# A slot-attention stage in new order: projections in other PSUM banks, ScalarE's and VectorE's queues rearranged

## The reference, cut to what matters

```
xn = layernorm(x);  q, k, v = rope(xn @ Wq), rope(xn @ Wk), xn @ Wv
sk = clip(xn @ sk_w1 @ sk_w2 + sk_b2, -32, 32);  wk = exp(sk);  zk = cumsum(wk over time)
sv = clip(xn @ sv_w1 @ sv_w2 + sv_b2, -32, 32);  wv = exp(sv);  zv = cumsum(wv over time)
logits = (causal(q k^T) @ wk) * scale / zk;      p = softmax(logits over the 64 slots)
o = causal((p / zv) @ wv^T) @ v
g = xn @ Wg;   on = o * rsqrt(mean(o*o) + eps) * gnorm_w
x = x + (on * g * sigmoid(g)) @ Wo
```

## Time and profile before

| | us |
|---|---|
| time of the kernel, median of 3 runs (lowest, highest) | 1716.53 (1711.35, 1729.82) |
| the profiled execution's own time | 1712.71 |
| its span, first to last instruction | 1710.9 |
| first stage, up to its last instruction | about 302.4 of 1710.9 |
| PE busy over the span | 1504.7 (88%) |
| ScalarE, VectorE, GpSimd busy | 1257.0, 1190.1, 530.2 |

### The profile page before, as it was taken

How to read it: one execution, slowest core, us unless ns; L and a number is a source line. 1 busy time by engine, 2 the same in 40 slices (tenths; PEclk the granted TensorE clock), 3 DMA queues, 4 the chain that set the end, 5 groups by cost and what they waited for, 6 DMA issues and landing times. The chain is left out here.

```text
span 1710.9 us, 37885 instructions
## 1 busy us (share of the span) xinstructions
PE 1504.7 (88%) x14142; PEld 724.0 (42%) x14142; DVE 1190.1 (70%) x1933; ACT 1257.0 (73%) x2113; POOL 530.2 (31%) x908
## 2 busy tenths in 40 slices
PE   7889987774699999998889999978874999999998
PEld 4666666662133333336633333345541333333356
DVE  4778777798999999967710000047878999999743
ACT  4654563697488888885689999926663888888863
POOL 3422342552323333334400010022221333333362
PEclk9999998797699999999999999989986999999999
DMA  4000000025434444420133333211333333333211
GB/s 132 1 1 2 1 2 1 1 82 166 142 102 111 107 110 111 107 62 27 45 89 98 94 100 97 66 36 39 99 108 113 84 91 89 89 92 92 67 38 38
DMA packets 140411, 125.42 MB, mean 73 GB/s; under 512 B 38411, under 2 KB 118341, under 8 KB 140229
## 3 DMA queue, kind: packets, MB, share of 16 engines
q1 hardware_dynamic: 130980, 121.90, 24.6%
q0 software_dynamic: 8192, 0.77, 0.9%
q10 hardware_dynamic: 1056, 0.33, 0.1%
HBM read 77.19 MB, written 44.96 MB: 71 GB/s over the span
## 5 line engine op out<-in xcount | busy, mean ns | idle before, releaser
L1700 ACT ACTIVATE m_probs<-m_psum 128x512 f32<-128x512 f32 (+1 forms) x768 | 511.6, 761 | 60.9 <-PE m_psum L1623 59.9
L1700 ACT ACTIVATE e_probs<-e_psum 128x512 f32<-128x512 f32 x512 | 276.4, 596 | 53.6 <-PE e_psum L1623 52.0
L1740 DVE TENSOR_REDUCE a_minus_max<-m_psum 128x2 f32<-128x1024 f32 x256 | 300.8, 1218 | 14.4 <-PE m_psum L1632 13.1
L1740 DVE TENSOR_REDUCE a_minus_max<-e_psum 128x2 f32<-128x1024 f32 x256 | 300.5, 1218 | 14.8 <-PE e_psum L1632 13.3
L1623 PE MATMUL m_psum<-m_q_stack,m_k_stack 114*32 114x512 bf16 (+1 forms) x4096 | 294.3, 384 | 6.6 <-DMA m_k_stack<-n_parts 4.4
L1643 PE MATMUL m_psum<-m_probs,m_v_ones 128*32 128x512 f32 x2048 | 269.5, 599 | 3.9 <-DVE m_pair L1690 2.6
L1623 PEld LDWEIGHTS m_psum<-m_q_stack,m_k_stack 114*32 114x32 bf16 (+1 forms) x4096 | 106.4, 96 | 224.2 <-issue 124.6
L1623 PE MATMUL e_psum<-e_q_stack,e_k_stack 126*32 126x512 bf16 x2048 | 157.5, 384 | 2.3 <-ACT e_probs L1700 2.2
L1643 PE MATMUL e_psum<-e_probs,e_v_ones 128*32 128x512 f32 x1024 | 132.2, 593 | 0.0
L1632 PE MATMUL m_psum<-m_k_stack,m_q_stack 48*128 48x512 bf16 x512 | 93.2, 400 | 31.8 <-DVE a_minus_max L1740 24.3
L1632 PE MATMUL e_psum<-e_k_stack,e_q_stack 60*128 60x512 bf16 x512 | 93.9, 400 | 29.4 <-DVE a_minus_max L1740 23.6
(11 more groups left out here) (402 smaller groups left out, 2630.3 us busy)
## 6 DMA issues: line engine op xcount, KB each, us to landing
polar_q<-m_late SPq DMA_DIRECT2D x24, 256.0 KB, 3.0
polar_k<-m_late SPq DMA_DIRECT2D x24, 256.0 KB, 3.2
m_q_stack<-polar_q SPq DMA_DIRECT2D x64, 96.0 KB, 2.3
m_k_stack<-polar_k SPq DMA_DIRECT2D x64, 96.0 KB, 2.4
ctx<-a_context_pairs SPq DMA_DIRECT2D x48, 128.0 KB
a_context_pairs<-slot_w SPq DMA_DIRECT2D x24, 256.0 KB, 2.2
m_q_stack<-dist_parts SPq DMA_DIRECT2D x192, 32.0 KB
m_k_stack<-dist_parts SPq DMA_DIRECT2D x192, 32.0 KB
```

The source lines that it names most:

```text
L1700: act.activation(self.buf.probs[(NT * m + c) % self.buf.PROBS][:, self.WIDE * part:self.WIDE * (part + 1), :], self.ps_s[i % self.PAIRS], ...
L1740: dve.tensor_reduce(self.minus_max[n % 2][:, k:k + NT + 1:NT], self.ps_r[r % self.TWOS], AX.X, ALU.max, negate=True).then_inc(self.two_fre ...
```

## The change: what it does

Banks: projections 1 and 3 use bank 7, projections 0 and 2 bank 4; "low" uses bank 7, "gT" bank 4; the slot matmuls stay in 0 to 3, but all four belong to batch s (lag 0). PE: in each step, projections 1 and 0 come right after `attend`, projections 3 and 2 between the two halves of the logits, `low` ahead of `outputs`, slots 1 and 0 after `mean_squares`, slots 3 and 2 after `project_out`, and the gate's matmul last. A step opens with the key sums; `turn_q` goes ahead of `turn_k`; the transposes of the norm go behind `turn_values`. ScalarE: the logarithm and the copy of the first key sums come first in the step, ahead of the softmax's exponential; then the copies of q and k, the values' logarithm and inverse, and behind these the four gate activations (the sigmoid is split into methods of its own, with the same instructions); the four qkv copies and the low copy come before `square`; the four exponentials of w end the step. VectorE: the clips move to the end of the step before, `gate_product` behind the third state copy, the statistics of the next batch between `key_newton` and `scale_logits`, `apply_gate` ahead of `add`, the second scan to the very end. GpSimd's and SyncE's queues are as before. No instruction is added or dropped.

```diff
@@ -1938,12 +1938,18 @@
-    def gate_sigmoid(self, act, b):
+    def gate_exponential(self, act, b):
         act.wait_ge(self.g_steps, 3 * b + 1)
         act.activation(sig[:, :], sig[:, :], ACT.Exp, scale=-1.0, bias=self.consts[:, 1:2]).then_inc(self.g_steps, 1)
+
+    def gate_logarithm(self, act, b):
+        sig = self.sig[b % 2]
         act.wait_ge(self.g_steps, 3 * b + 2)
         act.activation(sig[:, :], sig[:, :], ACT.Ln, bias=self.sv.ones[:, 0:1]).then_inc(self.g_steps, 1)
+
+    def gate_sigmoid(self, act, b):
+        sig = self.sig[b % 2]
         act.wait_ge(self.g_steps, 3 * b + 3)
         act.activation(sig[:, :], sig[:, :], ACT.Exp, scale=-1.0).then_inc(self.sig_ready, 1)
...
-        slot = SlotAttention(nc, sv, tag, norm, last_slot=3)
+        slot = SlotAttention(nc, sv, tag, norm, last_slot=2)
         banks = Banks(nc, tag, 8, (
-            ("slot2", 2, 1, (slot.clip_done[2],)), ("slot3", 3, 1, (slot.clip_done[3],)), ("zk0", 5, 1, (slot.zk_ready[0],)),
-            ("state1", 7, 1, (slot.state_ready[1],)), ("kT", 5, 1, (slot.kT_ready,)), ("qT", 6, 1, (slot.qT_ready,)),
+            ("zk0", 5, 1, (slot.zk_ready[0],)), ("state1", 7, 1, (slot.state_ready[1],)), ("kT", 5, 1, (slot.kT_ready,)), ("qT", 6, 1, (slot.qT_ready,)),
...
-            ("L1", 6, 1, (slot.lg_ready[1],)), ("L0", 5, 1, (slot.lg_ready[0],)), ("proj1", 1, 0, (slot.qkv_ready[1],)),
-            ("o", 4, 2, (slot.on_ready,)), ("proj0", 0, 0, (slot.qkv_ready[0],)), ("wvT1", 6, 1, (slot.wvT_ready[1],)),
-            ("ms", 5, 2, (slot.ln_ready,)), ("out", 6, 3, (slot.x_done,)), ("proj3", 3, 0, (slot.qkv_ready[3],)), ("proj2", 2, 0, (slot.qkv_ready[2],)),
-            ("low", 4, 0, (slot.lowT_ready,)), ("gT", 5, 0, (slot.gated_ready,)), ("slot1", 1, 0, (slot.clip_done[1],)), ("slot0", 0, 0, (slot.clip_done[0],))))
+            ("proj1", 7, 0, (slot.qkv_ready[1],)), ("proj0", 4, 0, (slot.qkv_ready[0],)), ("L1", 6, 1, (slot.lg_ready[1],)),
+            ("proj3", 7, 0, (slot.qkv_ready[3],)), ("proj2", 4, 0, (slot.qkv_ready[2],)), ("L0", 5, 1, (slot.lg_ready[0],)), ("low", 7, 0, (slot.lowT_ready,)),
+            ("o", 4, 2, (slot.on_ready,)), ("wvT1", 6, 1, (slot.wvT_ready[1],)), ("ms", 5, 2, (slot.ln_ready,)),
+            ("slot1", 1, 0, (slot.clip_done[1],)), ("slot0", 0, 0, (slot.clip_done[0],)), ("out", 6, 3, (slot.x_done,)),
+            ("slot3", 3, 0, (slot.clip_done[3],)), ("slot2", 2, 0, (slot.clip_done[2],)), ("gT", 4, 0, (slot.gated_ready,))))
         norm.banks = slot.banks = banks
...
         for s in STEPS:
             for b in batch(s, 1):
-                slot.slot(pe, b, 2)
-                slot.slot(pe, b, 3)
                 slot.key_sums(pe, b, 0)
                 slot.states(pe, b, 1)
+                slot.turn_q(pe, b)
                 slot.turn_k(pe, b)
-                slot.turn_q(pe, b)
                 slot.states(pe, b, 2)
                 slot.scores(pe, b)
...
-            for b in batch(s, 0):
-                norm.turn(pe, b)
             for b in batch(s, 1):
                 slot.states(pe, b, 3)
                 slot.key_sums(pe, b, 1)
                 slot.turn_values(pe, b, 0)
+            for b in batch(s, 0):
+                norm.turn(pe, b)
             for b in batch(s, 2):
                 slot.attend(pe, b)
+            for b in batch(s, 0):
+                slot.project(pe, b, 1)
+                slot.project(pe, b, 0)
             for b in batch(s, 1):
                 slot.slot_logits(pe, b, 1)
+            for b in batch(s, 0):
+                slot.project(pe, b, 3)
+                slot.project(pe, b, 2)
+            for b in batch(s, 1):
                 slot.slot_logits(pe, b, 0)
             for b in batch(s, 0):
-                slot.project(pe, b, 1)
+                slot.low(pe, b)
             for b in batch(s, 2):
                 slot.outputs(pe, b)
-            for b in batch(s, 0):
-                slot.project(pe, b, 0)
             for b in batch(s, 1):
                 slot.turn_values(pe, b, 1)
             for b in batch(s, 2):
                 slot.mean_squares(pe, b)
+            for b in batch(s, 0):
+                slot.slot(pe, b, 1)
+                slot.slot(pe, b, 0)
             else:
                 for b in batch(s, 3):
                     slot.project_out(pe, b)
             for b in batch(s, 0):
-                slot.project(pe, b, 3)
-                slot.project(pe, b, 2)
-                slot.low(pe, b)
+                slot.slot(pe, b, 3)
+                slot.slot(pe, b, 2)
                 slot.gate(pe, b)
-                slot.slot(pe, b, 1)
-                slot.slot(pe, b, 0)
         folding.turn_ternary(pe, 0)
...
         for s in STEPS:
             for b in batch(s, 1):
-                slot.qkv_copy(act, b, 2)
-                slot.low_copy(act, b)
-                slot.gate_guard(act, b)
-                slot.gate_sigmoid(act, b)
-                slot.weights(act, b, 1)
-                slot.weights(act, b, 0)
+                slot.key_log(act, b, 0)
             for b in batch(s, 2):
                 slot.exponential(act, b)
             for b in batch(s, 1):
-                slot.weights(act, b, 2)
-                slot.key_log(act, b, 0)
+                slot.q_copy(act, b)
+                slot.k_copy(act, b)
             for b in batch(s, 2):
                 slot.value_log(act, b)
+                slot.value_inverse(act, b)
             for b in batch(s, 1):
-                slot.k_copy(act, b)
-                slot.q_copy(act, b)
+                slot.gate_guard(act, b)
+                slot.gate_exponential(act, b)
+                slot.gate_logarithm(act, b)
+                slot.gate_sigmoid(act, b)
             for b in batch(s, 0):
                 norm.normalise(act, b)
             for b in batch(s, 1):
-                slot.weights(act, b, 3)
-            for b in batch(s, 2):
-                slot.value_inverse(act, b)
-            for b in batch(s, 1):
                 slot.key_log(act, b, 1)
                 slot.values_copy(act, b, 0)
-                slot.key_inverse(act, b)
             for b in batch(s, 0):
                 norm.copy(act, b)
+            for b in batch(s, 1):
+                slot.key_inverse(act, b)
+            for b in batch(s, 0):
+                slot.qkv_copy(act, b, 1)
+                slot.qkv_copy(act, b, 0)
+                slot.qkv_copy(act, b, 3)
+                slot.qkv_copy(act, b, 2)
+                slot.low_copy(act, b)
             for b in batch(s, 2):
                 slot.square(act, b)
-            for b in batch(s, 0):
-                slot.qkv_copy(act, b, 1)
             for b in batch(s, 1):
                 slot.values_copy(act, b, 1)
             for b in batch(s, 2):
                 slot.inverse_rms(act, b)
             for b in batch(s, 0):
-                slot.qkv_copy(act, b, 3)
-                slot.qkv_copy(act, b, 0)
+                slot.weights(act, b, 1)
+                slot.weights(act, b, 0)
+                slot.weights(act, b, 3)
+                slot.weights(act, b, 2)
         folding.finish_proj(act)
...
+        norm.statistics(dve, 0)
+        norm.aggregate(dve, 0)
+        dve.wait_ge(constants, ALL_CONSTANTS)
+        dve.wait_ge(memsets, 3)
         for s in STEPS:
-            for b in batch(s, 0):
-                norm.statistics(dve, b)
-                norm.aggregate(dve, b)
-            if s == 0:
-                dve.wait_ge(constants, ALL_CONSTANTS)
-                dve.wait_ge(memsets, 3)
             for b in batch(s, 1):
-                slot.clip(dve, b, 1)
-                slot.clip(dve, b, 0)
-                slot.gate_product(dve, b)
-                slot.clip(dve, b, 2)
-            for b in batch(s, 2):
-                slot.scan(dve, b, 1)
-            for b in batch(s, 1):
-                slot.clip(dve, b, 3)
                 slot.state_copy(dve, b, 1)
...
             for b in batch(s, 1):
                 slot.state_copy(dve, b, 3)
+                slot.gate_product(dve, b)
                 slot.mask_scores(dve, b, 1)
                 slot.mask_scores(dve, b, 2)
             for b in batch(s, 2):
                 slot.mask_attention(dve, b, 1)
                 slot.mask_attention(dve, b, 2)
                 slot.mask_attention(dve, b, 0)
+                slot.mask_attention(dve, b, 3)
             for b in batch(s, 1):
                 slot.key_newton(dve, b)
+            for b in batch(s + 1, 0):
+                norm.statistics(dve, b)
+                norm.aggregate(dve, b)
+            for b in batch(s, 1):
                 slot.scale_logits(dve, b, 1)
-            for b in batch(s, 2):
-                slot.mask_attention(dve, b, 3)
...
                 slot.scan(dve, b, 0)
             for b in batch(s, 2):
                 slot.apply_rms(dve, b)
+            for b in batch(s, 0):
+                slot.clip(dve, b, 1)
+                slot.clip(dve, b, 0)
+            for b in batch(s, 2):
```

(8 more changed lines are left out.)

## The result

The changed kernel takes 1703.17 us (median of 8 runs, 1702.03 to 1704.43), the kernel before 1714.72 (8 runs): a ratio of 0.9923, 95% interval 0.9896 to 0.9949. The forecast was 1706, within 1696 to 1722, and less than 1% faster. The intervals of the ratios are 0.1 to 0.3% to either side, up to 5 us. So a difference between two of the variants further down rests on the length of the step in their traces, and the times only agree with it. The profiled span went from 1710.9 to 1701.6 us. The last instruction of the first stage, the sum at L2454 (L2460 in the changed file), starts at 301.68 before and at 290.21 after, 11.5 us earlier; the later groups gave back 2.2 in these two executions (9.3 in the whole span).

What follows compares the result with a forecast made beforehand. The prediction took PE's queue, with its waits, to bound the first stage's step. Its terms -2.1, -9.7 and +1.3 took 1712.71 to 1702.2 for the profiled execution; with 3.8 for the median it forecast 1706, range 1696 to 1722.

Steps and rivals of the forecast that it cites:

- The bound and the rope's wait: First stage: PE's queue sets the 33.54 us step; its 1.86 wait for GpSimd's rope ahead of `states` goes.
- The signs that the prediction named: Rope wait near 0, step 31.8 to 32.4, `attend` idle 0.4 to 0.8, `scores` waiting about 0.5, one scan over 1.3.
- Term (a): Steady step, start of `attend` to end of the next key sums: 22.0 - 0.55 + 0.26 = 21.7 us.
- Term (b): Steady step, end of key sums to `attend`: 10.36 us by the chain through softmax and masks, 1.2 less than before.
- The walk: The prediction's pass through one steady step in the new order with the old instruction lengths; period 32.1 us.
- Term (c): Step 2's `states` -2.1, on to step 8's `states` -9.7, there to `attend` +1.3, drain 0: -10.5 us.
- rival 3: No gain: ScalarE late by 2.2 us with the norm's copy, PE waiting at L1922 or L269; 1716, chance 0.15.
- The last step of the sum: Whole kernel: 1702.2 for the profiled execution, plus 3.8 for the median of the runs, gives 1706.
- Nothing for the clock in the steady steps: Steps 2 to 8: no separate clock term; the step of 34.67, inside the -9.7, would have no clock fall.
- Rival 1: Drain: the tail's clock stays up, saving 5.4 us; 1700.6, chance 0.15.
- Rival 2: Second half of step, VectorE's queue from `subtract` to clip 0 waits for whole GpSimd operations: 5.1 us, 1728; chance 0.10.

Runs made afterwards that it cites:

- third experiment: The changed kernel with the output projection ahead of slots 1 and 0 on PE: 1698.36 us, ratio 0.9904 to the kernel before.
- fourth experiment: The changed kernel with the softmax's exponential moved to the end of ScalarE's step before, ahead of the exponentials of w: 1698.18 us, ratio 0.9901.
- fifth experiment: The changed kernel with GpSimd's rope making two of its four products: 1702.15 us, ratio 0.9917 to the kernel before.
- seventh: The changed kernel with projections 3 and 2 behind both halves of the logits, not between them: 1711.90 us, ratio 0.9977.
- second experiment: The changed kernel with the gate's four activations back at the head of ScalarE's step, ahead of the key sums' logarithm: 1729.56 us, ratio 1.0084.
- eighth: The changed kernel with the rope's four products made twice on GpSimd: 1736.53 us, ratio 1.0116 to the kernel before.

## Why the prediction was right

- **The bound and the rope's wait.** Right, and shown alone: the old order with a short rope makes a step of 32.1. The signs that the prediction named came: no wait for the rope in the steady steps, 32.03, `attend` behind the last mask after 0.48, `scores` waiting 0.38, a scan of 1.55.
- **Term (a), `attend` to the end of the key sums.** Forecast 21.7. Measured 154.44 to 175.60: 21.16. The 0.55 went, though a gap of 0.30 is left between the gate's matmul and the key sums (third experiment). The 0.54 beyond the forecast was not foreseen. As much lies at the four projections: from start to start they took 3.30 before (0.86, 0.75, 1.39, and a gap of 0.30 ahead of `outputs`) and take 2.74 in two pairs (1.39, 1.35). By the timelines that gap was a wait for the fourth attention mask (L2227, 167.06 to 167.74 before), which VectorE now makes right behind the other three; no run changes this alone.
- **Term (b), key sums to `attend`.** Forecast 10.36, measured 143.57 to 154.44: 10.87. The chain is the one named, logarithm, copy, exponential, softmax, masks (fourth experiment). What failed is its first link, the logarithm 0.04 behind the key sums: it comes 0.69 behind them. The walk had the weights of slots 1 and 0 ready 1.5 us before PE asks; they are ready 0.05 before (173.99 against 174.04), and the two exponentials of slots 3 and 2, which stand ahead of the logarithm, come later still. The walk left out that `apply_rms` writes the one buffer og and so waits for the output projection. With that wait gone (third experiment) the part takes 10.25, a tenth under the forecast. The errors of (a) and (b) cancelled, 0.54 against 0.51: that 32.1 met 32.03 so closely is luck.
- **Term (c), the ends.** Forecast -2.1 - 9.7 + 1.3 = -10.5; measured +0.1 - 12.6 + 1.9 and -0.9 in the drain, so -11.5. This sum is nearer than its terms, which were off by +2.2, -2.9, +0.6 and -0.9.
  - `states` of step 2 starts at 49.84 instead of 49.75. The rope no longer holds it (from the key sums to it 1.40 and not 3.71), but step 1 takes 26.46 instead of 25.12: PE waits 1.28 at L1922 for ScalarE's copy of the norm, the sign of rival 3, and 1.34 for the weights. And step 1 begins 1.06 later, which is no doing of the order: in the ten traces its key sums start between 20.91 and 22.27, in either order.
  - From there to step 8 it is 189.75 us, not six times 32.1: in step 2 there is no output projection for `apply_rms` to wait for, and the step is 30.2, the next 31.3.
  - Step 8, `states` to `attend`, took 11.03 and not 10.5: its `attend` waits 1.16. The 0.9 of the drain lie at `outputs` of step 8, which stood idle for 0.99 before, again behind the fourth attention mask, and follows at once now.
- **The last step of the sum.** The forecast for the profiled execution was 1702.2, and it took 1703.43. The 3.8 us put on top, the distance of the median of three runs from the profiled one, did not hold: the median of eight runs of the kernel before is 1714.72, 2.0 above it, and the changed kernel's is 0.3 below its own.
- **Nothing for the clock in the steady steps.** Right: it is 1.00 in each of them. The kernel before had the lower level behind two of its seven rope waits in steps 2 to 8: the one of the earlier trace rows, and that of 2.14 in step 2:

```profile
46.30:79.80 33.50, 29.89 (x228) 21.93 (x227) 23.82 (x39) 18.44 (x33) 11.49 (x13) 0.95 0.01 1
```

- **Rival 1** did not come: the drain's clock is 0.72 as before, and PE waits 4.80 there. **Rival 3** came in step 1 only, as said; in the steady steps the first projection follows `attend` at once (156.43), and PE waits for ScalarE at `turn_k` and `scores` alone.
- **Rival 2**, the lock of VectorE and GpSimd, is real but asleep: `subtract` takes 1.42 instead of 1.22, the scan 1.55, and the rope 9.36 instead of the 7.54 of the walk, so that it ends 3.4 us ahead of `states` and not some 6. None of this reaches PE, for VectorE waits 1.70 behind it (fifth experiment). With the rope 2.3 us later it took much of the gain (seventh). I gave it 0.10; its place was right, its size depends on where the rope's last sum falls.
- **Left untested.** In the old order the rope's last sum met the second scan and took 2.20 instead of 1.27: 0.93 of the wait of 1.86 was this lock. The change moves that scan to the end of VectorE's step. The scan's move alone, in the old order, might have brought up to that much of the 1.51 a step; no run tries it. Nor does any run try the new banks by themselves.

By the Trainium skill (SBUF — State Buffer, "Who interferes with whom"), a VectorE instruction with two SBUF inputs contends with a GpSimd instruction that reads SBUF, and the shared pair of ports is an exclusive lock. The trace agrees: `apply_gate`, with two inputs in SBUF, takes 1.62 instead of 0.68 beside the rope's last sum (seventh experiment). The same section of the Trainium skill leaves `tensor_reduce` out of it; here `maximum`, which is one, took 1.22 beside the rope's products (164.85 in the changed kernel).

## What to carry to other kernels

When a wait stands out in a queue-bound step, ask first whether its producer can simply start earlier, and test it with a shortened producer: one run then prices that wait. It does not price the rearrangement that is to remove it, which wins and loses elsewhere too (here 1.00 and 0.94 a step against the shortened producer). Then list every wait of each instruction that moves, single buffers above all; the one left out here was worth 1.0 us a step, some 5 us in all. Slack against the consumer is not the whole slack: a helper engine that is early enough for its reader can still fall on a neighbour's two-input instructions.

## What the runs showed of the hardware that was not expected

- A stalled PE can cost more than its wait. Behind the 3.38 us of the second experiment and the 3.02 of the eighth matmuls run at the lower clock, and a step loses about a microsecond more (35.99 at a clock of 0.91 against 35.04 at 0.95, with the same wait; in the kernel before 34.67 against 33.54, behind the same wait of 1.86). The wait's length alone doesn't decide it: five of the seven rope waits in steps 2 to 8 of the kernel before, of 1.43 to 1.86, had no fall behind them. In the changed kernel the clock is 1.00 in every steady step.
- GpSimd's four products take 5.00 us beside clips and statistics, 5.98 beside `subtract`, and 6.96 where both `subtract` and the scan meet them: 0.98 for each such instruction.
